# Attention probabilities split by ScalarE and GpSimd and turned by DMA, with a new order of turns in the DMA queue

## The reference, cut to what matters

```python
q = query @ Wq + bq
kv = context @ Wkv + bkv                      # 77 context tokens, k and v, 16 heads of 32
scores = jnp.einsum('bhid,bhjd->bhij', q, k) * scale
scores = jnp.where(mask[:, None, None, :], -jnp.inf, scores)
attn = jax.nn.softmax(scores, axis=-1)
out = jnp.einsum('bhij,bhjd->bhid', attn, v)
out = out.transpose(0, 2, 1, 3).reshape(b, sq, d)
return out @ Wout + bout
```

## Time and profile before

| what | us |
|---|---|
| three executions | 1817.82, 1825.38, 1830.28 (median 1825.38) |
| the profiled execution | 1823.66 |
| its span in the profile | 1821.9 |
| PE busy | 1371.2 |
| DVE busy | 1421.6 |
| ACT busy | 692.5 |
| POOL busy | 243.9 |

### The profile page before, as it was taken

How to read it: one execution, slowest core, us unless ns; L and a number is a source line. 1 busy time by engine, 2 the same in 40 slices (tenths; PEclk the granted TensorE clock), 3 DMA queues, 4 the chain that set the end, 5 groups by cost and what they waited for, 6 DMA issues and landing times.

```text
span 1821.9 us, 24307 instructions
## 1 busy us (share of the span) xinstructions
PE 1371.2 (75%) x8120; PEld 705.4 (39%) x8120; DVE 1421.6 (78%) x2437; ACT 692.5 (38%) x2105; POOL 243.9 (13%) x197
## 2 busy tenths in 40 slices
PE   5044737799787978698778978797869886988663
PEld 4021315344453436344543345343634453434321
DVE  6988896878787687787787878768777778786695
ACT  2112206451455227441644146422734164425310
POOL 1102200131003200230013100320013001310000
PEclk9556868899889989999999989998999999999888
DMA  9175761042101420233004210142023300420012
GB/s 348 68 243 146 188 143 36 6 88 64 42 1 35 93 59 14 35 62 77 25 7 87 58 48 1 35 93 59 14 35 65 75 24 6 87 58 24 7 24 51
DMA packets 267433, 120.08 MB, mean 66 GB/s; under 512 B 244090, under 2 KB 244602, under 8 KB 265750
## 3 DMA queue, kind: packets, MB, share of 16 engines
q1 hardware_dynamic: 267286, 118.27, 26.5%
HBM read 49.04 MB, written 8.39 MB: 32 GB/s over the span
## 4 chain that ended last, share of the span: by engine, by line
issue 43%; DVE 26%; PE 18%; DMA 4%; SPq 4%; ACT 3%; POOL 2%; POOLq 0%; DVEq 0%; ACTq 0%
PE bank L1075 13%; PE bank L1164 5%; DVE amax L826 2%; DVE pair L835 2%; DVE hid L831 2%; SPq L314 2%; DVE th L868 2%; SPq L303 1%; DVE pair L850 1%; DMA region<-region 1%; ACT region L535 1%; DVE pair L843 1%; DMA hqt<-pair 1%; DVE sc L797 1%; DVE stats L686 1%
## 5 line engine op out<-in xcount | busy, mean ns | idle before, releaser
L1164 PE MATMUL bank<-w_dn,region 128*128 128x512 fp8e4 x1024 | 243.7, 386 | 40.0 <-DMA region<-region 40.0
L1075 PE MATMUL bank<-w_up,xt 128*128 128x512 fp8e4 x1024 | 248.6, 391 | 32.7 <-ACT region L499 17.4
L1075 PE MATMUL bank<-w_gate,xqt 128*128 128x512 bf16 x512 | 147.9, 416 | 122.2 <-DVE th L868 78.4
L508 ACT ACTIVATE th<-bank,half_cg 128x512 f32<-128x512 f32 x128 | 88.0, 687 | 350.2 <-PE bank L1075 350.2
L426 POOL TENSOR_TENSOR region<-g,region 128x512 f16<-128x512 f32 x128 | 178.9, 1402 | 300.9 <-ACT region L499 292.9
L868 DVE SCALAR_TENSOR_TENSOR th<-th,bank 128x512 f32<-128x512 f32 x128 | 87.6, 684 | 138.4 <-ACT th L508 138.3
L535 ACT ACTIVATE region<-bank,nm 128x77 f32<-128x77 f32 x512 | 160.0, 345 | 68.2 <-DVE nm L914 68.2
L1075 PE MATMUL bank<-w_down,hqt 128*128 128x512 bf16 x512 | 134.3, 422 | 56.9 <-DMA hqt<-pair 56.9
L496 ACT ACTIVATE g<-bank 128x512 f32<-128x512 f32 x128 | 76.4, 597 | 247.2 <-PE bank L1075 188.2
L1164 PEld LDWEIGHTS bank<-w_dn,region 128*128 128x128 f16 x1024 | 101.0, 99 | 167.4 <-issue 52.0
L1075 PEld LDWEIGHTS bank<-w_up,xt 128*128 128x128 f16 x1024 | 102.0, 101 | 163.5 <-issue 55.4
(11 more groups left out here) (206 smaller groups left out, 2473.6 us busy)
## 6 DMA issues: line engine op xcount, KB each, us to landing
xin<-in_x SPq DMA_DIRECT2D x16, 512.0 KB, 4.1
out_x<-x SPq DMA_DIRECT2D x16, 512.0 KB, 3.0
region<-in_w_up_t SPq DMA_DIRECT2D x1, 4096.0 KB, 12.9
hid<-in_gate_w SPq DMA_DIRECT2D x4, 1024.0 KB, 5.2
x<-in_gate_w SPq DMA_DIRECT2D x4, 1024.0 KB, 6.1
hid<-in_up_w SPq DMA_DIRECT2D x4, 1024.0 KB, 5.2
x<-in_up_w SPq DMA_DIRECT2D x4, 1024.0 KB, 5.8
hid<-in_down_w SPq DMA_DIRECT2D x4, 1024.0 KB, 4.9
```

The source lines that it names most:

```text
L508: eng.activation(th[:, u % 2, :], bank[4][:, :], ACT.Tanh, scale=half_cg[:, :]).then_inc(sg["th"], 1)
L1075: last = mm(out, lhs, rhs, start=(n == 0), stop=(n == len(pairs) - 1))
L1164: last = mm(bank[2 + t % 2][:, :], ht[i][:, t % 2, f, :], w_dn[:, f, :], start=(f == 0 and i == 0), stop=(f == KF - 1 and i == 1))
```

## The change

- The exponentials go to three p3 buffers, from three score banks (4, 5, 7), and drop `accum_out`.
- ACT copies p3 (SBUF, 128 x 308 f32) as the high part into `ps3`, POOL subtracts for the low part (`p_lo`), and one transposing DMA per item (`turn_p`, 128 x 1024 f16, as large as turn_x's) brings both parts into `pt3`. There are three ps3 and four pt3 buffers; two of the latter are the two halves of `th`.
- PE's f32 transposes (L1235), ACT's copies from PSUM (L526) and DVE's subtractions (L919) are gone.
- A column of ones beside each head's values makes the row sums: 12 products of 33 columns, in banks 2 and 6. DVE takes the reciprocals from PSUM and scales in two halves.
- The value products come at lag 5, not 4 (`PV_LAG`), and all steps of a tile behind them one step later (on3 6, ott and oth 7, otl 8, out3 9, x3 10).
- POOL's `sdev` stands after the low part of item 14, in n = 16.
- SP's order: 16 turn_p ahead of turn_x; turn_ht(1) ahead of turn_h(0), and turn_ht(3) ahead of turn_h(1).

```diff
-        pt3 = [region[:, at + i * 2 * HC * P:at + (i + 1) * 2 * HC * P].rearrange("p (r h t) -> p r h t", r=2, h=HC)
-               for i in range(2)]
+        p3 = f32_at(2 * KD * T, 3 * HC * M).rearrange("p (r h m) -> p r h m", r=3, h=HC)
+        turn_n = 2 * HC * P
+        ps3 = [region[:, at:at + turn_n] for at in (half - 2 * turn_n, half - turn_n, 2 * half - 2 * turn_n)]
+        pt3 = [region[:, at:at + turn_n] for at in (2 * half - 4 * turn_n, 2 * half - 3 * turn_n)]
+        pt3 += [th[:, i, :].bitcast(F16) for i in range(2)]
...
+            def turn_p(g, m):
+                want(sp, "p3l", g, m + 1)
+                sp.sem_inc(sm["sp_passed"])
+                if m >= 4:
+                    want(sp, "o3", g, m - 3)
+                    sp.sem_inc(sm["sp_passed"])
+                sp.dma_start_transpose(pt3[m % 4].rearrange("p i h t -> p (i h) t"),
+                                       ps3[m % 3].rearrange("p i h t -> p (i h t)")).then_inc(sg[f"pt{m % 4}"], 16)
...
             def turns(g, g1, g2):
+                for m in range(TILES * NC):
+                    turn_p(g, m)
                 for h in range(2):
                     turn_x(g, h)
                 if g1 is not None:
                     turn_ht(g1, 0)
+                    turn_ht(g1, 1)
                 turn_h(g, 0)
                 if g1 is not None:
-                    turn_ht(g1, 1)
                     turn_ht(g1, 2)
+                    turn_ht(g1, 3)
                 turn_h(g, 1)
-                if g1 is not None:
-                    turn_ht(g1, 3)
                 store(g, 0)
...
+            def p_lo(g, m):
+                want(pool, "p3h", g, m + 1)
+                eng.tensor_tensor(ps3[m % 3][:, 1, :, 0:M], p3[:, m % 3], ps3[m % 3][:, 0, :, 0:M],
+                                  ALU.subtract).then_inc(sg["p3l"], 1)
             def phase_a(g3, g1):
+                for n in range(STEPS):
+                    if g3 is not None and 2 <= n <= TILES * NC + 1:
+                        p_lo(g3, n - 2)
+                    if n == VAR2_AT + 1 and g1 is not None:
+                        want(pool, "var2", g1)
...
-                    eng.activation(pt3[0][0:M, m % 2], bank[6 + m % 2][0:M, :].rearrange("p (h t) -> p h t", h=HC),
-                                   ACT.Copy).then_inc(sg["p3h"], 1)
                 if n < TILES * NC:
                     want(act, "nm3", g, n + 1)
+                    if n >= 3:
+                        want(act, "p3l", g, n - 2)
                     for j in range(HC):
+                        last = eng.activation(p3[:, n % 3, j, :], scores(n)[:, j * M:(j + 1) * M], ACT.Exp,
+                                              bias=nm3[:, n % 3, j:j + 1])
+                if 1 <= n <= TILES * NC:
+                    m = n - 1
+                    want(act, "p3", g, m + 1)
+                    if m >= 3:
+                        want_pt(act, g, m - 3)
+                    eng.activation(ps3[m % 3][:, 0, :, 0:M], p3[:, m % 3], ACT.Copy).then_inc(sg["p3h"], 1)
...
-                    if n >= 2:
-                        want(pe, "p3", g, n - 1)
+                    if n == 2:
+                        want(pe, "nm3", g, 1)
+                    if n >= 3:
+                        want(pe, "p3", g, n - 2)
...
+                if PV_LAG <= n < TILES * NC + PV_LAG:
+                    m = n - PV_LAG
+                    want_pt(pe, g, m)
                     if c == 0 and t:
+                        want(pe, "on3", g, 2 * t)
                     for j in range(HC):
+                        hi, lo = (pt3[m % 4][0:M, i, j, :] for i in range(2))
+                        last = product(with_sums(h // 8)[:, h % 8, :], [(hi, vals1[0][:, b, h, :]), (hi, vals1[1][:, b, h, :]),
+                                                                       (lo, vals1[0][:, b, h, :])])
```

More of the change, by code:

```diff
@@ L100, in build @@
         keys1 = [sb(f"keys1{i}", [P, B, NC, HC, M], F16) for i in range(2)]
-        vals1 = [sb(f"vals1{i}", [M, B, D], F16) for i in range(2)]
+        vals1 = [sb(f"vals1{i}", [M, B, HEADS, HD + 1], F16) for i in range(2)]
         row_one = sb("row_one", [P, P], F16)
@@ L179, in build @@
         th = sb("th", [P, 2, D], F32)
+        pt3 += [th[:, i, :].bitcast(F16) for i in range(2)]
+        ps3, pt3 = ([a.rearrange("p (i h t) -> p i h t", i=2, h=HC) for a in w] for w in (ps3, pt3))
         NB = F // BLOCK
@@ L211, in build @@
                    up=16, g32=16, hh=16, hl=16, sq=16, ms=2, rms=2, ht_even=64, ht_odd=64, dn=4, x2=4,
-                   qp=4, q32=4, qh=4, ql=4, sc3=16, nm3=16, p3=16, p3t=16, p3h=16,
-                   p3l=16, o3=16, on3=4, ott=4, oth=4, otl=4, out3=4, x3=4,
+                   qp=4, q32=4, qh=4, ql=4, sc3=16, nm3=16, p3=16, p3h=16,
+                   p3l=16, pt0=64, pt1=64, pt2=64, pt3=64, o3=16, on3=8, ott=4, oth=4, otl=4, out3=4, x3=4,
                    xq=2, xqt=32, gu=16, th=16, gate=16, hg=16, hid=16, hq=4, hqt=64, dn4=4,
@@ L660, in _ @@
                     settle()
+            for i in range(2):
+                done(eng.memset(vals1[i][:, :, :, HD:HD + 1], 1.0 - i))
             for b in range(B):
@@ L663, in _ @@
                 settle()
[L664 removed]
+                split(vals1[0][:, b, :, 0:HD], vals1[1][:, b, :, 0:HD], sq[0:M, :].rearrange("p (h e) -> p h e", h=HEADS))
                 settle()
@@ L907, in attend @@
                         want(dve, "ott", g, t)
[L908 to L911 removed]
+                    for a in range(2):
+                        hs = slice(a * HEADS // 2, (a + 1) * HEADS // 2)
+                        done(eng.reciprocal(rr3[:, hs].unsqueeze(2), with_sums(a)[:, :, HD:HD + 1]))
+                    settle()
+                    for a in range(2):
+                        hs = slice(a * HEADS // 2, (a + 1) * HEADS // 2)
+                        eng.tensor_tensor(on3[:, :].rearrange("p (h e) -> p h e", h=HEADS)[:, hs], with_sums(a)[:, :, 0:HD],
+                                          rr3[:, hs].unsqueeze(2).to_broadcast([P, HEADS // 2, HD]),
+                                          ALU.mult).then_inc(sg["on3"], 1)
                 if n < TILES * NC:
                     want(dve, "sc3", g, n + 1)
[L914 removed]
+                    eng.tensor_reduce(nm3[:, n % 3, :], scores(n)[:, 0:HC * M].rearrange("p (h m) -> p h m", h=HC),
                                       AX.X, ALU.max, negate=True).then_inc(sg["nm3"], 1)
[L916 to L926 removed]
+                t = tile_at(n, 8)
                 if t is not None:
@@ L1237, in attend @@
-                t = tile_at(n, 6)
+                t = tile_at(n, 7)
                 if t is not None:
-                    want(pe, "on3", g, t + 1)
+                    want(pe, "on3", g, 2 * t + 2)
                     if t:
```

76 lines of the change are left out of this document (16 added, 60 removed).

## The result

The changed kernel is **slower**: 1845.35 us (median of four, 1842.66 to 1847.02) beside 1821.6 us, a ratio of 1.012 (95% interval 1.009 to 1.016). I had forecast 1749 and a range of 1728 to 1800, and given 0.10 to slower. The span of the profiled execution is 1840.6 us, before 1821.9.

The account below looks back on a forecast made before the run. PE was taken to bound the attention, ACT and DVE close behind, and DVE behind x3(3). Gains of 10.4 us a phase, 72.8 over seven, and 4 in the last group gave 1749 us; range 1728 to 1775, with half-way to 1800.

Parts of the forecast that it names:

- S3 to S15: Second attention, from scores of item 3 to those of item 15: 23.4 us for 28.34, a gain of 4.9.
- S15 to T0: From item 15's scores to the first transposition of the next group's second norm: 7.1 us for 9.11, gain 2.0.
- T0 to x3(3): First transposition of next group's second norm to DVE's addition for last tile: two moves cancel, 0 (-1.7 to +1.7).
- S0 to S3: From the second attention's first scores to those of item 3: 5.5 us, not 7.8, gain 2.3 (0 to 3.1).
- So PE stays the bound: In the 12-item stretch of the attention, PE, busy 26.05 of 28.34 us before, still sets the pace.
- the ring: ACT's copy waits for the DMA landing three items earlier: 1.53 us an item; rival that this bounds, slower: 0.07.
- x3(3) to gate_up(1): Behind DVE's addition for the last tile: the last quantising step now runs ahead of it, gain 0.6 (0 to 0.7).
- SP's order: PE's 0.7 us wait for turned tile 1 goes with turn_ht(1) first: gain 0.6 a phase (0 to 0.7).
- The clock rival: With PE less busy, its clock falls to 1.2 GHz in attend: +38 us over the loop, 1869; chance 0.03.
- POOL beside DVE: DVE's scaling after sdev beside POOL's subtraction: up to 0.8 us later, some 6 over the loop; counted as nothing.
- The last group, gain 4: Last group, without stage1: ACT sets 1.69 us an item, then about 1.55; gain 4 us (-3 to +8).
- The half-way rival: PE, ACT and DVE wait for each other in fixed orders: only 6.0 us a phase, 1781 us; chance 0.16.

Follow-up runs that it names:

- e6: The aligned kernel: changed kernel with first attention's tiles 2 and 3, second norm, first up products and quantising of x4(0) one step later; 1780.44 us, ratio 0.974.
- e2: Changed kernel with PV_LAG 4 and all attention lags back to those of the kernel before; 1806.2 us, ratio 0.990.
- e11: Changed kernel with only the quantising of x4(0) one step later (VAR4_AT); 1823.15 us, ratio 1.002.
- e13: Kernel before with the last part of the quantising of x4(0) one step earlier, ahead of x3(3); 1821.97 us, ratio 1.000.
- e4: Changed kernel with the old order of turn_ht and turn_h in the DMA queue; 1846.29 us, ratio 1.011.
- e8: Changed kernel with added products, into columns that nothing reads, to keep PE at work where it idled in the attention; 1828.86 us, ratio 1.004.
- e7: Changed kernel with the chain behind on3 (ott, oth, otl, out3, x3) back one step, value products and on3 still late; 1792.52 us, ratio 0.985.
- e12: Changed kernel with only the last part of the quantising of x4(0) one step later, behind x3(3); 1835.67 us, ratio 1.006.
- e3: Kernel before with ott, oth, otl, out3 and x3 one step later, value products and on3 unmoved; 1892.14 us, ratio 1.037.

## Why the prediction was wrong, step by step

Per loop phase I had added up a gain of 10.4 us; measured is a loss of 2.1. Of this miss of 12.5 us the step S3 to S15 has 5.4, S15 to T0 4.1 and T0 to x3(3) 2.1. The three have one fault in common: a moved step was priced by its own work and the chain behind it, not by what it now stands ahead of in its engine's queue.

- *S0 to S3, gain 2.3*: right, 2.7.
- *S3 to S15, gain 4.9*: wrong, a loss of 0.5, and the largest miss. "So PE stays the bound" failed, with "if the waits of 2.3 us stay": PE's busy time without the transpositions came out as worked out (20.4 us at the full clock, in the row of e6 above; I had 20.3), but it stood idle 5.5 us of those 25.9, and 6.1 of the 30.5 in the changed kernel. The costs under it were right (POOL 0.75, landing 3.1, the ring no bound; ACT's copy takes 0.35 us start to start where I took 0.31), and an item in which nothing else meets does go at 1.33 to 1.47 us in the aligned kernel (1071.17, 1072.64, 1073.97 for three starts). But I used 0.48 us per item as if all items were alike. The stretch is long by its exceptional items, at tile ends and stage1's steps: from scores to scores the longest item takes 4.22 us in the kernel before and 4.29 in the changed one, the shortest 1.68 and 1.31. With the order repaired the stretch is 26.5 us, a gain of 2.2; what is left of the 4.9 no run gained.
- *S15 to T0, gain 2.0*: wrong, a loss of 2.1. I followed only the chain of item 15 and not out3(1) and x3(1), which the lags had moved between S15 and the second norm on PE and DVE.
- *T0 to x3(3), "two moves cancel"*: wrong, and with the most runs against it. It had a bound of 1.7 us and lost 2.1; moving the order back (e2) or along (e6) brings 4.0 to 4.2. That the x3 of one tile, the norm and up share DVE's and PE's queues was in my text; that out3(2) would run at the low clock (3.51 us, 2.76 before) was not.
- *x3(3) to gate_up(1), gain 0.6*: 0.3 by the mean, and given back right behind it, as "rest" grew by 0.3 (its first block alone by 2.3) where the SP order was to take 0.6 off. "That wait of PE is worth nothing alone" was wrong in its sign: removing it costs the clock of the next block (e11, and the block in e13, though there it is made up elsewhere).
- *SP's order, gain 0.6*: nothing (e4). The landing: right. The ring of 1.53 us an item was not reached as a bound: in the aligned kernel three items in a row take 1.48, 1.47 and 1.33 us.
- *The clock rival*, at 0.03: I refused it since PE would be 86% busy. It was 80%, and the granted clock fell to 0.83 to 0.88 there, the one of my signs of being wrong that clearly came. It did not halve throughout, and the rival's 1869 us is far off, but undoing a part of it is worth some 15 us net (e8), and PE's matmuls are in flight 7.1 us a group longer than in e6. The sum also had no term for the clock behind x3(3), where the block from gate_up(1) took 5.83 us for 3.47.
- *POOL beside DVE, counted as nothing*: right, as I had said, because they do not meet. None of the 96 executions of L748 (the L718 of before) overlaps work of POOL; each takes at most 0.547 us, as before the change. So the rule of the Trainium skill (GPSIMD Engine Reference, Key points), that the two contend in some modes, was not tried at this place. The row that I gave for it does agree with it: in the kernel before, all 14 executions of L856 beside POOL's L426 take 1.366 to 1.373 us, all 18 others 0.531 to 0.545.
- *The last group, gain 4*: 1.1 by the profiled spans. "ACT sets 1.69 us an item" was read from one item; S3 to S15 there is 23.2 us, 1.94 an item, and 22.7 after.
- *The half-way rival* (1781) had the right idea, that fixed orders limit an item, and stopped at no loss.

In sum: with the new division the kernel is 1.0 to 1.5% faster than before in two orders (e2, e7) and 2.6% with everything moved together (e6). The order of the changed kernel costs 3.8% against the last (ratios 1.012 and 0.974), by waits and by the low clock together. I treated a delay of one step as latency that is hidden; in a program with in-order queues it is a new order.

What stays open: how the gain of e6 divides between division and order, since a kernel before with everything one step later (PV and on3 too) was not run; how the cost of the order divides between waits and clock; and what sets which groups of e12, and of e6, go the fast way.

## What to carry to other kernels

In a hand-written software pipeline, a step that moves by one slot should be listed with all steps of the same slot on each engine, old and new; where it passes one, name who waits for that one. If a chain must be one step later, move its neighbours with it, or keep only the part late that needs it (here PV and on3), and test the lags alone in the old kernel, all of those that the change moves: e3, which moved only some of them, showed at 66 us how dear a moved step can be. And a busy average per item is not its period: find the exceptional items first.

## What the runs showed of the hardware

- Removing a wait made the following code slower: behind 10.01 us of idle time in one piece the next block had a mean granted clock of 0.59 (5.83 us for 3.46). With idle pieces of 5.89 and 1.30 us (e11) the low clock fell on a block between them, in time that was idle otherwise, and the next one took 3.46.
- With 16 more transposing DMAs a group, at a DMA share of 0.65 to 0.77 in the attention, the new ones landed in 3.1 us in the median and 4.9 at most, the one of the same size before in 3.1 and 3.5. DVE's maximum of 308 columns stayed at 0.47 to 0.48 us, and PE's three score products at 0.56 at the full clock.
- DVE's scaling of 128 x 512 (f32 to f32) (L856, kernel before) takes 1.37 us beside POOL's subtraction L426, in 14 of 14 executions, and 0.54 in the 18 others.
